# Narrow passes of a graph kernel: 15 instead of 18 columns through TensorE, 13 instead of 10 gathers, and two of the five one-hot blocks made by ScalarE

## The reference

```python
# layer 0: m = tanh(x[src] * edge_weight);  segment_sum(m, dst)
# layer 1: attention: e2 = (ef @ W_attn + b) * x[src], softmax over the edges of each dst,
#          ft = segment_sum(e1 * attn, dst).sum(axis=1)
# layer 2: h = segment_max(x[src] * timestamp, dst);  h @ W.T + b
# layer 3: twice: agg = segment_sum(x[src], dst); h = relu(((1+eps)*x + agg) @ wa + ba) @ wb + bb
#          then log_softmax
x = _layernorm(x + layer(x), axis=-1)      # after each layer
```

## Time and profile before

| | |
|---|---|
| median of three runs | 8114.27 us |
| span of the profiled execution (first to last instruction) | 8106.3 us |
| what lies around the span (median less span) | 8.0 us |
| TensorE busy | 7107.4 us, 88% |
| VectorE busy | 6896.2 us, 85% |
| GpSimd busy | 5221.6 us, 64% |
| ScalarE busy | 2239.6 us, 28%, nearly all of it in the attention |
| mean granted TensorE clock | 0.956 |

### The profile page before, as it was taken

How to read it: one execution, slowest core, us unless ns; L and a number is a source line. 1 busy time by engine, 2 the same in 40 slices (tenths; PEclk the granted TensorE clock), 3 DMA queues, 4 the chain that set the end, 5 groups by cost and what they waited for, 6 DMA issues and landing times.

```text
span 8106.3 us, 209725 instructions
## 1 busy us (share of the span) xinstructions
PE 7107.4 (88%) x77871; PEld 6661.2 (82%) x77871; DVE 6896.2 (85%) x12224; ACT 2239.6 (28%) x7389; POOL 5221.6 (64%) x4570
## 2 busy tenths in 40 slices
PE   5999985999999999999995399998599996899994
PEld 5999984777777787777774399998599996899994
DVE  7999985999999999999997688888588885788884
ACT  0000003666666666666664100000000000000000
POOL 3555557888888888888886555555555555455554
PEclk9999997999999999999997699999799998899997
DMA  2223222555555555555554211111111111111110
GB/s 84 85 87 88 84 56 81 159 158 159 159 160 160 160 160 160 159 158 158 159 160 134 65 49 46 48 49 40 36 49 45 49 49 28 43 49 49 49 45 22
DMA packets 738222, 757.28 MB, mean 93 GB/s; under 512 B 153760, under 2 KB 698336, under 8 KB 738112
## 3 DMA queue, kind: packets, MB, share of 16 engines
q1 hardware_dynamic: 592640, 667.34, 24.9%
q0 software_dynamic: 140528, 86.77, 7.1%
q10 hardware_dynamic: 5008, 2.59, 0.1%
HBM read 239.80 MB, written 519.73 MB: 94 GB/s over the span
## 4 chain that ended last, share of the span: by engine, by line
PE 42%; DVE 29%; issue 23%; POOL 4%; DMA 1%; DVEq 1%; ACT 0%; ACTq 0%; another core or an unknown queue 0%; POOLq 0%; SPq 0%
PE ps L823 42%; DVE amax_room L1232 7%; DVE spare L1237 4%; DVE flat L1259 3%; DVE flat L954 2%; POOL got L456 2%; DVE msg L1137 2%; DVE stt L954 2%; DVE spare L1241 1%; DVE run L1158 1%; DVE wide_buf L954 1%; DVE raw L954 1%; POOL wide_buf L456 1%; DVE junk L1164 1%; DVE wide_buf L1116 1%
## 5 line engine op out<-in xcount | busy, mean ns | idle before, releaser
L456 POOL DMA_INDIRECT msg<-feat,cidx x1680 | 1681.5, 1001 | 1594.4 <-PE ps L823 1109.8
L823 PE MATMUL ps<-parts,wide_buf 128*128 128x160 bf16 x30240 | 2128.9, 233 | 289.0 <-DVE wide_buf L1116 276.4
L823 PEld LDWEIGHTS ps<-parts,wide_buf 128*128 128x128 bf16 x30240 | 2102.5, 98 | 304.8 <-issue 288.2
L456 POOL DMA_INDIRECT hsrc<-feat,aidx x1568 | 1921.5, 1225 | 461.1 <-issue 445.5
L823 PE MATMUL ps<-parts,flat 128*128 128x160 bf16 x30240 | 2118.5, 233 | 29.7 <-DVE flat L1116 16.7
L823 PEld LDWEIGHTS ps<-parts,flat 128*128 128x128 bf16 x30240 | 2093.3, 98 | 43.1 <-DVE flat L1116 21.4
L870 PEld LDWEIGHTS ps<-wsb,zT 102*128 102x128 f32 x9408 | 1462.9, 190 | 217.8 <-ACT zT L690 196.3
L870 PE MATMUL ps<-wsb,zT 102*128 102x192 f32 (+1 forms) x9408 | 1539.8, 313 | 99.0 <-ACT zT L690 98.5
L954 DVE TENSOR_TENSOR raw<-ps,amask 128x960 f32<-128x960 f32 x448 | 738.4, 1657 | 468.1 <-PE ps L823 286.5
L1137 DVE TENSOR_REDUCE msg<-raw 128x288 f32<-128x2880 f32 x224 | 1129.9, 5044 | 7.7
L657 ACT ACTIVATE cidx<-sidx 128x10 int32 (+1 forms) x224 | 46.8, 211 | 3684.6 <-DMA msg<-feat,cidx 3065.6
(11 more groups left out here) (220 smaller groups left out, 5229.9 us busy)
## 6 DMA issues: line engine op xcount, KB each, us to landing
state_tab<-flat SPq DMA_DIRECT2D x784, 512.0 KB
raw<-quot_tab SPq DMA_DIRECT2D x224, 576.0 KB
run_tab<-run SPq DMA_DIRECT2D x224, 224.0 KB
top_tab<-spare SPq DMA_DIRECT2D x392, 128.0 KB
msg<-feat,cidx POOLq DMA_INDIRECT x1680
hsrc<-feat,aidx POOLq DMA_INDIRECT x1568
efs<-in_ef SPq DMA_DIRECT2D x392, 34.0 KB
msg<-in_x,cidx POOLq DMA_INDIRECT x560
```

What stands on the lines that cost most here:

```text
L456: return pool.indirect_dma_start(dest, None, table, rows_at(idx))
L823: last = nc.tensor.matmul(block.rearrange("p (q c) -> p q c", c=D), hot[s][:, m, t * P:(t + 1) * P], parts[:, m * Q:(m + 1) * Q, part, :], ...
```

## The change

R goes from 18 to 15, OWN from 6 to 9, and so A from 10 to 13: TensorE has 225 matmuls in a group instead of 270, GpSimd 13 gathers instead of 10, and `pick` is incremented 13 times. The 15 columns lie in three own banks for each buffer (nine columns) and two shared ones (six). VectorE makes three of the five one-hot blocks (`HM` = 3); ScalarE makes blocks 3 and 4, each with two activations over 1920 elements: |quot - m| into the new tile `apart`, then relu(1 - that) into the block. TensorE waits for both (`hot` and the new semaphore `rest`). The candidates of one feature now lie side by side (`c q` in place of `q c`), in `parts`, in PSUM and in `picked`, so that the sum over candidates reads neighbours.

```diff
-R = 18
-OWN = 6
+R = 15
+OWN = 9
+HM = MB - 2
-        parts = sb("parts", [P, MB * Q, 3, D], BF)
+        parts = sb("parts", [P, MB, 3, D, Q], BF)
+        apart = sb("apart", [P, R * P], BF)
-        picked = raw[...].rearrange("p (r q c) -> p r q c", q=Q, c=D)
+        picked = raw[...].rearrange("p (r c q) -> p r c q", q=Q, c=D)
-        mine_banks = [ps[:, 2 * s:2 * s + 2, 0:CB * QW] for s in range(2)]
-        shared = ps[:, 4:8, 0:CB * QW]
+        mine_banks = [ps[:, BANKS * s:BANKS * (s + 1), 0:CB * QW] for s in range(2)]
+        shared = ps[:, 2 * BANKS:8, 0:CB * QW]
...
# ScalarE, new
+            def block(s, m):
+                if parted[0]:
+                    act.wait_ge(s_apart, parted[0])
+                nc.scalar.activation(apart[:], quot[:, s, :], ACT.Abs, bias=count[:, m:m + 1], scale=-1.0).then_inc(s_apart, 1)
+                parted[0] += 1
+                act.wait_ge(s_apart, parted[0])
+                ins = nc.scalar.activation(hot[s][:, m, :], apart[:], ACT.Relu, bias=1.0, scale=-1.0)
...
+                return ins.then_inc(q["rest"][s], 1)
...
+            def narrow_group(n, j, s, hots, indices, first=False):
+                if hots:
+                    differences(n, j + s, 1 - s, first)
+                    for m in range(HM, MB - 1):
+                        block(1 - s, m)
+                if n == 0:
+                    act.wait_ge(q["mul"][s], j + 1)
+                    nc.scalar.activation(val[:, s], val[:, s], ACT.Tanh).then_inc(q["act"][s], 1)
+                if indices:
+                    act.wait_ge(q["got"][s], (n * HALF + j + 1) * (16 * A))
+                    next_indices(2 * j + 2 + s, s)
+                if hots:
+                    block(1 - s, MB - 1)
...
# TensorE
                     pe.wait_ge(q["hot"][s], done + j + 1)
+                    pe.wait_ge(q["rest"][s], done + j + 1)
...
# VectorE
-                    for m in range(MB):
+                    for m in range(HM):
                         last = v.tensor_scalar(hot[s][:, m, :], quot[:, s, :], count[:, m:m + 1], None, ALU.is_equal)
...
-                    hold(v.tensor_reduce(msg[:, s, A:U, :], picked.rearrange("p r q c -> p r c q"), AX.X, ALU.add))
+                    hold(v.tensor_reduce(msg[:, s, A:U, :], picked, AX.X, ALU.add))
```

More of the change, by code:

```diff
@@ L285, in gnn_program @@
         s_share = sem("s_share")
-        NARROW = ("idx", "quot", "hot", "pick", "read", "got", "mul", "act", "run", "put")
+        s_enter = sem("s_enter")
+        s_apart = sem("s_apart")
+        s_count = sem("s_count")
+        NARROW = ("idx", "quot", "hot", "rest", "pick", "read", "got", "mul", "act", "run", "put")
         narrow = {k: ring(f"n_{k}") for k in NARROW}
@@ L342, in narrow_pass @@
                 sp.wait_ge(q["hot"][0], done + 1)
+                sp.wait_ge(q["rest"][0], done + 1)
                 load_quot(2, 0)
@@ L657, in next_indices, with differences @@
                 nc.scalar.activation(cidx[:, s, :], sidx[:, bass.ds(g * U, A)], ACT.Copy).then_inc(q["idx"][s], 1)
-            def index_round(n, j):
-                for s in range(2):
+            def differences(n, j, s, first, ready=True):
+                act.wait_ge(q["quot"][s], 16 * (n * HALF + j + 1))
+                if not first:
+                    act.wait_ge(q["pick"][s], (n * HALF + j) * A)
+                if ready:
+                    act.wait_ge(q["rest"][1 - s], n * HALF + j + s)
@@ L661, in index_round, with narrow_pass @@
                     act.wait_ge(q["got"][s], (n * HALF + j + 1) * (16 * A))
                     next_indices(2 * j + 2 + s, s)
-            def index_pass(n):
+                if hots:
+                    block(1 - s, MB - 1)
+            def narrow_pass(n):
                 for s in range(2):
                     next_indices(s, s)
[L667 to L675, removed]
-                    nc.scalar.activation(val[:, s], val[:, s], ACT.Tanh).then_inc(q["act"][s], 1)
@@ L678, in _ @@
-            act.wait_ge(s_sidx, 16)
-            for s in range(2):
-                next_indices(s, s)
-            with act.Fori(0, HALF - 1) as j:
-                tanh_round(j)
-            tanh_round(HALF - 1, False)
+                apart_start()
+                if n < 2:
+                    act.wait_ge(s_enter, n + 1)
+                differences(n, 0, 0, n == 0, n > 0)
+                for m in range(HM, MB):
+                    block(0, m)
+                if n == 0:
+                    apart_start()
+                    narrow_group(0, 0, 0, True, True, True)
+                    narrow_group(0, 0, 1, True, True)
@@ L684, in _ @@
+                with act.Fori(1 if n == 0 else 0, HALF - 1) as j:
+                    apart_start()
+                    for s in range(2):
+                        narrow_group(n, j, s, True, True)
+                apart_start()
+                narrow_group(n, HALF - 1, 0, True, False)
+                narrow_group(n, HALF - 1, 1, False, False)
+            act.wait_ge(s_sidx, 16)
+            act.wait_ge(s_count, 1)
+            narrow_pass(0)
             asked(st3[:], st2[:], ACT.Sqrt)
```

62 lines of the change are left out of this document (38 added, 24 removed).

## The result

The changed kernel takes **10166.69 us** (median of 4 runs, 10166.2 to 10177.48) where the kernel before took 8113.88 us on the same chip: a ratio of **1.2534 [1.2517, 1.2552]**. Forecast were 9560 us with a range of 9050 to 9780, so the direction was right and the size was short by 607 us. The profiled execution took 10166.7 us, its span 10164.7.

The account below looks back on a forecast made before the run. The prediction took TensorE to bound the narrow passes. Passes 1 to 3 would add 1012 us and pass 0 438, together 1450 on a span of 8106.3 with 8.0 around it: 9564, predicted as 9560 us, range 9050 to 9780.

Parts of the forecast that it names:

- The mechanism of the gaps: Between groups: last gather, copy of the indices, ScalarE's block 4, then TensorE's start; pass 0 also waits for the tanh.
- The bound by TensorE before: In the kernel before, narrow passes: TensorE sets the pace, 18.81 us a group in pass 1, 19.76 in pass 0.
- The clock: TensorE's clock falls in each gap, so every group starts cold and loses 2.3 us.
- the sentence on GpSimd: GpSimd's 13 gathers at 1.25 us take 16.3 us in a group, under the period.
- The gap: TensorE idle between groups, waiting for ScalarE's block 4: 7.1 us in passes 1 to 3, 9.9 in pass 0.
- the landing: From the start of a group's last gather until it has landed and ScalarE's copy starts: 2.4 us.
- from the copy to TensorE: ScalarE's copy of the indices and block 4's two activations, until TensorE starts the next group: 4.2 us.
- T + 0.5: Start of a group's last gather, 0.5 us after T, the end of the group's last matmul.
- T + 0.05: In pass 0, VectorE starts reading the shared banks 0.05 us after the end of the group's last matmul.
- Rival A: Gaps between groups come, but TensorE's clock stays up or returns at once: 9080 us, chance 0.10.
- B: ScalarE's activations on narrow types cost 0.7 us instead of 1.85, gaps 4.8 and 7.6 us: 9060 or 8800 us, chance 0.05.
- Rival C: Gathers are not last at a group's end, TensorE remains the bound, groups 15.6 to 16.3 us: 7550 us, chance 0.04.

Follow-up runs that it names:

- the late run: The changed kernel with 18 columns on TensorE and 10 gathers, block 4 left behind the copy of the indices and the tanh: 10222.82 us, ratio 1.2604.
- block 4 early: The changed kernel with block 4 of the next group made right behind block 3, ahead of the copy of the indices: 8712.98 us, ratio 1.0737.
- the run without a pace: The changed kernel with GpSimd issuing its gathers without waiting for TensorE's counts: 11091.52 us, ratio 1.3672.

## Why the prediction fell short

**The mechanism of the gaps was right, and a second one was missing.** The gaps are there, released by ScalarE's `relu`, and come from the order of block 4: undone, they go (8713 us); alone, they make 2115 us. The bound by TensorE before holds in passes 1 to 3; in pass 0 TensorE also waits 0.6 us a group for VectorE's blocks.

**The sum, term by term.** Worked out from the passes of the trace of after (225 matmuls as 15.56 us; the clock is what is left of a group's matmuls without the stalls):

| over the four passes, us | forecast | measured | off by |
|---|---|---|---|
| gaps | 544.5 + 3 x 390.5 = 1716 | 2029 | +313 |
| stalls inside a group | 0 | 349 | +349 |
| clock | 224 x 2.3 = 515 | 453 | -62 |
| sum | | | +600 |

The clock's term holds when it is counted apart: 31 of a group's matmuls follow each other at 0.13 us instead of 0.07, 444 us in all. The sum of +600 is close to the whole difference, 602.7 us between 9564 and the profiled 10166.7, partly by luck: outside the passes 15 us came on top where the prediction has 0, and off go 6 us since passes 2 and 3 were longer before than pass 1, and 6 us since only 2.0 us lie around a span. (The 8.0 was the median less the span of a single execution that was shorter than the median.)

*The step that failed* is the sentence on GpSimd: "13 x 1.25 = 16.3 us in a group, also under the period". As time on GpSimd that is right, as a cost it isn't. GpSimd's gathers were priced as if they lay beside TensorE for nothing because they fit. Issued 1.25 us apart they take TensorE's time: 349 us of stalls, by a term that the prediction puts at nothing. The trace of before had little to warn of it: 0.3 us a group of stalls inside the groups of pass 0, where gathers for the attention's slices come beside the ten, against 0.1 in passes 1 to 3. Most of the microsecond between 19.76 and 18.81 is another thing, VectorE's late blocks; the prediction took both as rates, and pass 0 as bound by TensorE alone, without asking.

*The gap* is the second step, mis-sized by 313 us: forecast at 7.1 and 9.9 us, it is 8.6 and 11.4 on average (1400 us in 162 gaps, 629 in 55). The price of each link held: 2.35 us for the landing (2.4), 4.07 from the copy to TensorE (4.2), and in pass 0 the sum at 2.65 (2.6). What was off in passes 1 to 3 is the place of the last gather, T + 1.6 instead of T + 0.5 in the gap shown, 1.4 us late on average; in pass 0 it is VectorE's reading, at T + 2.2 instead of T + 0.05. The prediction let GpSimd lag by its own rate of 1.25 against counts at 1.20; in the trace the counts themselves come late and in bursts. At ten gathers (the late run) the same working gave the gap to half a microsecond; so this term too is the density, in another place. How TensorE's signals get late is not shown by any run.

*The clock*, forecast at 2.3 us a group, was 2.0. In the trace of before it fell some 5.0 and 3.1 us behind the last matmuls of passes 0 and 1, and was then at 0.50 (1202 to 1208, 5656 to 5660); the gaps of 11.4 and 8.6 us on average are longer. That groups start cold behind such gaps each time was the author's estimate from single ones, and is borne out, by 0.50 in the gap shown and 0.54 up to 5655, and by the 31 slow matmuls a group. The run with filler matmuls bears out the price, 1.6 to 1.9 us a group, and shows that a filler beside gathers can cost as much as it brings: at a mean clock of 0.929 the ratio was 1.2624, not under 1.2534.

*Rival A* (the clock stays up) and *B* (cheap activations) were wrong by the clock rows and by 1887 ns. *Rival C* (faster, 7550 us) had the price of the order right in kind, but couldn't be had either: with the order undone, the split alone ends at 8713 us. C takes the gathers as free too: its 7550 us, and the 7500 to 7750 us expected of the run with block 4 early, miss the measured time by some 1000 us or more.

*On the transfer's size.* From the start of the last gather to the copy that waits for its landing it takes 2.46 us in the median of 41 groups with block 4 early (2.35 in the gap shown above), and 2.20 with 16 partitions instead of 128 (41 groups too). An eighth of the rows saves 0.26 us of it: most of the landing is fixed for each transfer, and so, by the ratios of 1.0737 and 1.0706, is most of the harm to TensorE.

## What to carry to other kernels

Work given to GpSimd as indirect DMAs is not free because GpSimd has room: price it by how far apart the transfers start, and look for "issue" stalls of TensorE beside them; here 1.9 us apart cost 0.1 us a group, 1.2 us apart 4.9. A wait that paces GpSimd by TensorE's progress can be what keeps TensorE fed, so don't remove it for slack. And where an engine does its work in the order in which it is written, as ScalarE here (`abs` of block 4 starts at 5646.48, behind the copy of 5646.36, which had waited 19.44 us), a block that the next group needs stands ahead of anything that waits for the end of this one: the same two instructions, one place later, cost 2115 us in the run with the old split.

## What the runs showed of the hardware

- Indirect DMAs issued back to back by GpSimd (0.95 us and 0.30 to the next) cut TensorE to one to three matmuls of 160 columns in a microsecond (5999 to 6008 of the run without a pace, the granted clock at 0.50), instead of seven at that clock (0.13 us each) or fourteen at 1.00 (0.07); the kernel before, without its pace, loses 25% by it (ratio 1.2486).
- The cost goes by the transfers and how close together they start, and not by their rows (ratio 1.071 with 16 partitions, 1.074 with 128) nor by GpSimd's being busy (0.969 with fills in the place of three gathers, 0.960 with nothing there).
- Making three matmuls one cut the number of stalls to a third (1485 to 498) and doubled their length (0.56 to 1.2 us); by distances, 4.9 us a group became 2.9.
- With 13 gathers VectorE's reading starts 2.2 us behind the recorded end of the last matmul in the median group; with 10 gathers and the same order, at most 0.25 us in three groups of four.
- An activation over 1920 elements from 16-bit to 16-bit numbers costs 1.80 to 1.89 us, and 2.12 to 2.22 over 2304, 0.92 to 0.98 ns an element against 0.95 for float32: by these traces narrow types save ScalarE nothing. A sum over neighbouring float32 numbers took 1.1 ns an element, over numbers 16 apart 1.75.
